# A gated post-norm layer on eight cores: one multiply-add of the inner norm moves from VectorE to ScalarE, and the row sums of the last norm move between the final down-projection blocks

## The reference

```
# layer 0, per batch; x is (4, 2048, 2048), sequence first, width second
q = x @ Wq;  v = x @ Wv;  lam = sigmoid(beta)       # 16 heads of 128
states[t] = lam * states[t-1] + v[t]                # scan over the sequence
y = (q * states)
y = (y - mean(y)) * rsqrt(var(y) + 1e-5) * ln_g + ln_b
y = y * silu(x @ Wg)
x = layernorm(x + y @ Wo)
h = silu(x @ Wgate.T) * (x @ Wup.T)                 # 8192 wide
x = layernorm(x + h @ Wdown.T)
```

## Time and profile before

| | us |
|---|---|
| median of 3 runs | 2291.34 (2288.99 to 2291.59) |
| the profiled execution | 2289.33 |
| its span, slowest core (core 0) | 2287.7 |
| spans of the 8 cores | 2276.5 to 2287.7 |
| TensorE busy, share of span | 1907.5, 83% |
| VectorE busy | 578.0, 25% |
| ScalarE busy | 343.0, 15% |

### The profile page before, as it was taken

The page is one execution under the profiler, slowest core; times in us unless marked ns, Lnnn a source line. Parts: engine busy times, 40 slices in busy tenths (PEclk is TensorE's granted clock), DMA queues, the critical chain, the costliest instruction groups (busy, mean ns, idle before and its releaser), DMA issues.

```text
span 2287.7 us, 25245 instructions; the slowest of 8 cores (2276.5 to 2287.7 us)
## 1 busy us (share of the span) xinstructions
PE 1907.5 (83%) x9751; PEld 970.2 (42%) x9898; DVE 578.0 (25%) x1351; ACT 343.0 (15%) x402; POOL 110.3 (5%) x230
## 2 busy tenths in 40 slices
PE   4898999921776469999999999999999999997640
PEld 2346864400554334444444444444444444443220
DVE  4222234578324521000110111111111111111154
ACT  0100015400001112222112112112111211200002
POOL 1000000000000000000000000000000000000000
PEclk9999999955878779999999999999999999999775
DMA  7651333430042034446435435434444443422303
GB/s 118 121 92 27 67 58 72 71 77 0 1 91 76 19 56 74 77 81 118 75 56 92 74 56 101 82 56 93 74 74 74 82 82 59 92 37 37 72 2 147
DMA packets 32453, 161.04 MB, mean 70 GB/s; under 512 B 3668, under 2 KB 3668, under 8 KB 22100
## 3 DMA queue, kind: packets, MB, share of 16 engines
q0 software_dynamic: 29744, 142.62, 34.8%
q1 hardware_dynamic: 2596, 16.79, 1.9%
HBM read 293.62 MB, written 8.39 MB: 132 GB/s over the span
## 4 chain that ended last, share of the span: by engine, by line
PE 79%; DVE 10%; DMA 5%; issue 3%; ACT 2%; DVEq 0%; POOL 0%; ACTq 0%; POOLq 0%; SPq 0%
PE p L1055 19%; PE p L1086 19%; PE p L1149 19%; PE p L492 5%; PE p L590 5%; PE p L966 5%; PE p L370 4%; DMA warena<-wd_t 2%; DMA bbuf<-x_loc 2%; DVE sqscr L788 1%; DVE sqscr L790 1%; DMA warena<-wo 1%; DVE qbuf L797 1%; DVE sqscr L792 1%; DVE mscr L1204 1%
## 5 line engine op out<-in xcount | busy, mean ns | idle before, releaser
L1055 PE MATMUL p<-tbuf,warena 128*128 128x512 bf16 x2006 | 461.8, 380 | 10.1 <-DMA warena<-wgu_t 7.9
L1086 PE MATMUL p<-tbuf,warena 128*128 128x512 bf16 x2006 | 460.2, 379 | 2.2
L1073 ACT ACT_TABLE_LOAD x128 | 164.2, 1283 | 1015.3 <-PE p L1055 1015.3
L1055 PEld LDWEIGHTS p<-tbuf,warena 128*128 128x128 bf16 x2048 | 200.8, 98 | 250.7 <-issue 10.4
L1086 PEld LDWEIGHTS p<-tbuf,warena 128*128 128x128 bf16 x2048 | 200.4, 98 | 241.6
L966 PE MATMUL p<-warena,qbuf 128*128 128x256 bf16 x1024 | 153.2, 303 | 135.8 <-DVE bbuf L980 80.0
L1149 PE MATMUL p<-warena,vbuf 128*128 128x512 bf16 x1005 | 228.6, 387 | 37.0 <-DMA warena<-wd_t 34.7
L1149 PE MATMUL p<-warena,qbuf 128*128 128x512 bf16 x1004 | 221.1, 379 | 1.1
L1165 DVE TENSOR_TENSOR bbuf<-bbuf,p 128x512 bf16<-128x512 bf16 x128 | 88.1, 688 | 397.0 <-PE p L1149 397.0
L966 PEld LDWEIGHTS p<-warena,qbuf 128*128 128x128 bf16 x1024 | 109.2, 107 | 181.1 <-issue 146.2
L1149 PEld LDWEIGHTS p<-warena,vbuf 128*128 128x128 bf16 x1024 | 101.2, 99 | 163.7 <-issue 48.0
(11 more groups left out here) (125 smaller groups left out, 731.4 us busy)
## 6 DMA issues: line engine op xcount, KB each, us to landing
warena<-wgu_t POOLq DMA_DIRECT2D x128, 512.0 KB, 6.8
warena<-wd_t POOLq DMA_DIRECT2D x32, 1024.0 KB, 13.6
warena<-wq POOLq DMA_DIRECT2D x8, 1024.0 KB, 9.1
warena<-wv POOLq DMA_DIRECT2D x8, 1024.0 KB, 9.2
warena<-wg POOLq DMA_DIRECT2D x8, 1024.0 KB, 8.3
warena<-wo POOLq DMA_DIRECT2D x8, 1024.0 KB, 17.6
sscr<-x_loc SPq DMA_DIRECT2D x8, 1024.0 KB, 4.8
out_loc<-sscr SPq DMA_DIRECT2D x8, 1024.0 KB, 4.3
```

Source lines behind the costliest of these rows:

```text
L1055: inst = t.matmul(p[gbk][:, 0:NT], warena[:, (j % 2) * GUSL + k * OPW + ot * 128: (j % 2) * GUSL + k * OPW + (ot + 1) * 128], tbuf[:, k * ...
L1073: inst = sc.activation(sscr[:, SIL_OFF + (gg % 2) * NT: SIL_OFF + (gg % 2 + 1) * NT], p[gbk][:, 0:NT], AF.Silu)
L1086: inst = t.matmul(p[ubk][:, 0:NT], warena[:, (2 + j % 2) * GUSL + k * OPW + ot * 128: (2 + j % 2) * GUSL + k * OPW + (ot + 1) * 128], tbuf ...
```

## The change

In the y2 stage the third operation of each group, `tmp * ln_g + ln_b`, is no longer a VectorE instruction but a ScalarE activation of the function Identity with a scale and a bias per partition. It reads `tmp` and writes a second buffer `tmp2`, which lies behind `tmp` in the same scratch tile `sqscr`; the tile's size works out the same as before (2048 columns). The gate multiply waits for ScalarE. The first multiply of a group no longer waits for VectorE's own last instruction, but for the activation of the group before.

The row sum and the sum of squares of the last norm are written by a new function `emit_ln3A(ci)`, called in `emit_down` right behind the last addition to block `ci`, instead of in a loop behind all of the down projection.

```diff
     first_y2 = [True]
+    prev_y2 = [None]
...
                     v.wait_ge(sS, mil[("gsil", ggrp)])
-                    v.wait_ge(sV, cnt["V"])
+                    if prev_y2[0] is not None:
+                        v.wait_ge(sS, mil[("y2t3", prev_y2[0])])
...
                     tick(v.tensor_mul(tmp, ysl, p[n2][:, 0:NT]), "V")
                     v.wait_ge(sV, cnt["V"])
-                    tick(v.tensor_add(tmp, tmp, p[2 + n2][:, 0:NT]), "V")
-                    v.wait_ge(sV, cnt["V"])
-                    tick(v.tensor_scalar(tmp, tmp, lngb[:, dt:dt + 1],
-                                         lngb[:, KT + dt:KT + dt + 1],
-                                         ALU.mult, ALU.add), "V")
-                    v.wait_ge(sV, cnt["V"])
+                    mil[("y2t2", ggrp)] = tick(
+                        v.tensor_add(tmp, tmp, p[2 + n2][:, 0:NT]), "V")
+
+                @blk.scalar
+                def _(sc, dt=dt, n2=n2, ggrp=ggrp):
+                    sc.wait_ge(sV, mil[("y2t2", ggrp)])
+                    tmp = sqscr[:, 0:2 * NT].bitcast(F32)
+                    tmp2 = sqscr[:, 2 * NT:4 * NT].bitcast(F32)
+                    mil[("y2t3", ggrp)] = tick(
+                        sc.activation(tmp2, tmp, AF.Identity,
+                                      bias=lngb[:, KT + dt:KT + dt + 1],
+                                      scale=lngb[:, dt:dt + 1]), "S")
+
+                @blk.vector
+                def _(v, dt=dt, n2=n2, ggrp=ggrp):
+                    v.wait_ge(sS, mil[("y2t3", ggrp)])
...
-                    inst = v.tensor_mul(ysl, tmp, gsl)
+                    inst = v.tensor_mul(ysl, tmp2, gsl)
...
+    def emit_ln3A(ci):
+        mc = 64 + ci * 8
+
+        @blk.vector
+        def _(v, ci=ci, mc=mc):
+            v.wait_ge(sV, mil[("dacc", NWIN - 1, ND - 1, ci)])
+            inst = v.tensor_reduce(mscr[:, mc:mc + 1],
+                                   bbuf[:, ci * D:(ci + 1) * D], AX.X, ALU.add)
+            mil[("l3rs", ci)] = tick(inst, "V")
...
+            inst = v.scalar_tensor_tensor(sqscr[:, 0:D], bsl, 1.0, bsl,
...
                 bank_r[bk] = ("V", cnt["V"])
+            if w == NWIN - 1 and n == ND - 1:
+                emit_ln3A(ci)
...
-    for ci in range(NCH):
-        mc = 64 + ci * 8
-
-        @blk.vector
-        def _(v, ci=ci, mc=mc):
-            if ci == 0:
-                v.wait_ge(sV, mil["ffn_done"])
-            inst = v.tensor_reduce(mscr[:, mc:mc + 1],
...
```

More of the change, by code:

```diff
@@ L97, in build_program @@
     zT = sbuf("zT", [128, KT * H], BF16)
-    sqscr = sbuf("sqscr", [128, max(2 * TOK, D)], BF16)
+    sqscr = sbuf("sqscr", [128, max(2 * TOK, D, 4 * NT)], BF16)
     mscr = sbuf("mscr", [128, 128], F32)
@@ L789, in _ @@
                     v.wait_ge(sV, cnt["V"])
-                    tick(v.tensor_add(tmp, tmp, p[2 + n2][:, 0:NT]), "V")
-                    v.wait_ge(sV, cnt["V"])
-                    tick(v.tensor_scalar(tmp, tmp, lngb[:, dt:dt + 1],
-                                         lngb[:, KT + dt:KT + dt + 1],
-                                         ALU.mult, ALU.add), "V")
-                    v.wait_ge(sV, cnt["V"])
+                    mil[("y2t2", ggrp)] = tick(
[12 more added lines that the diff above has]
+                    v.wait_ge(sS, mil[("y2t3", ggrp)])
+                    ysl = qbuf[:, dt * TOK + n2 * NT: dt * TOK + (n2 + 1) * NT]
+                    tmp2 = sqscr[:, 2 * NT:4 * NT].bitcast(F32)
                     gsl = bbuf[:, dt * TOK + n2 * NT: dt * TOK + (n2 + 1) * NT]
-                    inst = v.tensor_mul(ysl, tmp, gsl)
+                    inst = v.tensor_mul(ysl, tmp2, gsl)
                     mil[("y2", ggrp)] = tick(inst, "V")
+                prev_y2[0] = ggrp
                 if n2 == NN2 - 1:
@@ L1002, in build_program, with _ @@
         return dbg_finish()
+    def emit_ln3A(ci):
[6 more added lines that the diff above has]
+            mil[("l3rs", ci)] = tick(inst, "V")
+        @blk.vector
+        def _(v, ci=ci, mc=mc):
+            v.wait_ge(sV, cnt["V"])
+            bsl = bbuf[:, ci * D:(ci + 1) * D]
+            inst = v.scalar_tensor_tensor(sqscr[:, 0:D], bsl, 1.0, bsl,
+                                          ALU.mult, ALU.mult,
+                                          accum_out=mscr[:, mc + 1:mc + 2])
+            mil[("l3sq", ci)] = tick(inst, "V")
     NSLOT = 2 * WINP
```

## The result

| | before | after |
|---|---|---|
| median of 8 runs, us | 2291.67 | 2320.37 |
| ratio | 1 | 1.0113 (1.0094 to 1.0131) |
| span of the profiled execution, us | 2287.7 | 2312.4 |
| y2 stage, first multiply to first copy, us | 97.6 | 140.2 |
| first of the last additions to the last sum, us | 61.9 | 43.6 |

Some runs on either side were disturbed by a slower clock on one die; the ratio leaves them out, the medians do not (without them they are 2291.47 and 2316.64). The forecast was 2316.1 and +24.8 us; the ratio gives +26 (21.5 to 30), and the spans of the two profiled executions 24.7. Of these 42.6 come from the y2 stage and -18.3 from the last norm's sums.

What follows compares the result with a forecast made beforehand. The chain was taken as 79% TensorE and 10% VectorE, with the y2 stage and the closing sums exposed on VectorE. +43.5 us there and -18.7 us in the sums gave +24.8, hence 2316.1 us, range 2306 to 2330.

Steps and rivals of the forecast that it cites:

- The stage is on the path in full: y2 stage: a serial VectorE chain of 97.6 us that nothing hides; the change adds 43.5 us to the total.
- A load in each block, behind the wait: y2 stage: each of 32 new ScalarE blocks loads its table after the wait, 1.29 us from load to activation.
- Rival A: y2 stage: no load spent on Identity, or done while VectorE works; total 2274.8 us, faster; chance 5%.
- The activation: y2 stage: Identity on 128x512 fp32 with scale and bias from memory takes 0.82 us, bounds 0.60 and 0.93.
- The hand-overs and the removed wait: y2 stage: VectorE to ScalarE 0.08 us, back 0.11; next multiply starts 0.61 us after the gate multiply.
- The sums: Last norm: VectorE sets a pace of 5.39 us a block, and the sums end 18.7 us earlier.
- Nothing in between: Between y2 stage and tail: nothing reordered on TensorE, POOL or SP; costed at 0.
- B: y2 stage: extra blocks stall the queues, one late step per group, 11.5 us more, 2327.6 us; chance 7%.
- C: Last column block: TensorE, waiting a third of the time, gets a lower clock; +8.7 us, 2324.8; chance 4%.
- D: y2 stage: each load brings about its own length again beyond its 1.28 us; 42 us higher, 2358; chance 2%.
- no second group in flight: y2 stage: gate multiply stands ahead of the next group's multiply, so VectorE sits still while ScalarE works; 4.39 us a group.

Runs made afterwards that it cites:

- experiment 1: Changed kernel with the last norm's sums put back in their loop behind the down projection, so only the y2 change remains; ratio to before 1.0182, median 2332.0 us.
- experiment 3: Changed kernel with the 32 Identity activations merged into one ScalarE block, every wait kept; ratio to the kernel before 0.9926.
- experiment 2: Kernel before with only the last norm's sums moved between the last additions, y2 stage as before; ratio 0.9917, median 2273.2 us.
- experiment 6: Changed kernel with y2 groups overlapped, their activations in one block, and the last norm's sums of squares on ScalarE; ratio to before 0.9722, lowest run 2231.99 us.
- Experiment 4: Changed kernel with the next y2 group's multiply and addition written ahead of the gate multiply, two buffers, all 32 loads kept; ratio to before 0.9817.
- experiment 7: On top of experiment 6, the last norm's small operations run once over 8 columns, one Sqrt instead of eight; ratio to before 0.963, lowest run 2210.26 us.

## Why the prediction was right

- **The stage is on the path in full.** Right: the longest wait of TensorE grew by 21.1 us (about 21.6 forecast), and the stage's 42.6 us appear in the time (experiment 1, +41.7). The sum had +43.5, because it took the stage before as 32 x 3.03 = 97.0 us where it is 97.6, and the stage after as 32 x 4.39 = 140.5 where it is 140.2.
- **A load in each block, behind the wait.** Right, and it was the deciding term: 32 loads of 1283 ns; experiment 3 removes 31 of them and 39.6 of the 42.6 us. Rival A's mechanism, no load spent on Identity, was as good as built there: 2274.6 to 2276.3 against the 2274.8 that was worked out for it.
- **The activation.** 0.812 us against 0.82. This fits 0.61 for 512 columns and 0.10 for each of two operands per partition, but no run takes the operands away, so that split is not shown.
- **The hand-overs and the removed wait.** 0.07, 0.10 and 0.61 us against 0.08, 0.11 and 0.61; a group 4.38 against 4.39.
- **The sums.** 5.40 us a block against 5.39, a gain of 18.3 in the trace and 19 in experiment 2 against 18.7. The one late step of 0.36 us accounts for most of the difference in the trace; experiment 2 has no such step and gains 18.6.
- **Nothing in between.** 24.7 in the spans less 42.6 - 18.3 leaves 0.4 us. That compares core 0 with core 2. The mean span of the 8 cores grew by 25.7 us, from 2282.2 to 2307.9, which leaves 1.4 us without an assigned cause. The stretch from the y2 stage to the last additions, though, lasts 1584 to 1591 us on different cores of the kernel before alone, so the executions do not show that anything was added there.
- **Rivals B, C and D.** The blocks did not stall the queues (one late step in the eight blocks of the tail, and one in the 32 groups, 2.64 us of waiting instead of 2.29); the granted clock was 1.00 from 2232 to 2248, with TensorE busy two thirds of the time; a load brought nothing beside its own 1.28. The row that the prediction reads for this under D, the Sqrt of the earlier trace rows, does not follow another function, though: ScalarE's last activation before it is the Sqrt of L748. A Sqrt behind a Silu is the first of the last norm, in the timeline of before:

```profile
2239.14 0.16 DVE L1232 TENSOR_TENSOR mscr<-mscr 128x1 f32<-128x1 f32 x1
2239.38 1.28 ACT L1239 ACT_TABLE_LOAD   x1 [194.40 <-DVE mscr L1232]
2240.68 0.29 ACT L1239 ACTIVATE mscr<-mscr,epsc 128x1 f32<-128x1 f32 x1
```

VectorE's operation ends at 2239.30, the load starts 0.08 later and the activation 1.30 after the load. ScalarE had been idle for 194 us there, which could hide something ahead of the load. In experiment 6 there is no idle time: the Sqrt's load starts at 2181.98, 0.01 behind the last Square. So the conclusion stands, by other rows than the one named.

The prediction also named the order of the queue, "no second group in flight", but priced only the round trip that follows from it. Experiment 4 shows how much lies in the order: with the same loads and hand-overs the stage is 64 us shorter than in the changed kernel.

## What to carry to other kernels

An operation moved to an idle engine need not take time off a chain whose next link waits for it. Here its time on ScalarE (0.81 us, against 0.55 on VectorE) and the hand-overs used up what was saved: 3.09 us a group without loads, against 3.03. The table loads came on top. Give the first engine something to do in between: write the next group's first operations ahead of the wait, on a second buffer. Where ScalarE's work is written in many blocks, count the loads in the trace; one block for a run of activations (experiment 3), or one activation over many columns (experiment 7), leaves one.

## What the runs showed of the hardware that was not expected

Interleaving alone cut VectorE's four operations from 3.03 to 2.26 us a group: dependent steps of 0.79 us (0.69 of work) became 0.60, and an instruction that does not wait for the one just before it starts about 0.09 before that one ends. The Trainium skill (VectorE: DVE Perf Modes, "The DRAIN you can't avoid") says that leaving out the semaphores between chained operations gains nothing, though an instruction that is not held (in the page's own sense of the word) starts earlier, and its "Rules for kernel authors" advise fewer operations. No run here drops a semaphore. What the runs show is that it matters which instruction the wait is for: 0.79 us from start to start where it is for the one just ahead, 0.60 where it is for an older one. Every operation and its wait stayed, only the order and the second buffer are new, and a quarter of the stage was gone.

An activation with an accumulated output is followed by an instruction of its own, 0.19 us on ScalarE (experiment 6), and 128x2048 columns without operands per partition took 1.91 us.
